# Two of every 32 tiles of gathered rows are replaced by column copies on VectorE and ScalarE

## The reference

```python
msg_in = concat([nodes[src], nodes[dst], edge_features])        # 64 + 64 + 32
messages = relu(msg_in @ mW1 + mb1) @ mW2 + mb2                 # 160 -> 128 -> 64
aggregated = segment_sum(messages, dst, num_segments=12500)
y = relu(concat([nodes, aggregated]) @ uW1 + ub1) @ uW2 + ub2   # 128 -> 128 -> 64
return layernorm(nodes + y)
```

## Time and profile before

| what | value |
|---|---|
| median of 3 runs | 2034.05 us |
| the profiled execution, its own time | 2035.36 us |
| its span | 2033.6 us |
| mean granted TensorE clock | 0.785 |
| busy: PE, DVE, ACT, POOL | 1408.9, 872.2, 557.6, 1488.3 us |
| DMA | 173.50 MB, 85 GB/s |

### The profile page before, as it was taken

The page is one execution under the profiler, slowest core; times in us unless marked ns, Lnnn a source line. Parts: engine busy times, 40 slices in busy tenths (PEclk is TensorE's granted clock), DMA queues, the critical chain, the costliest instruction groups (busy, mean ns, idle before and its releaser), DMA issues.

```text
span 2033.6 us, 34717 instructions
## 1 busy us (share of the span) xinstructions
PE 1408.9 (69%) x10080; PEld 1283.7 (63%) x10080; DVE 872.2 (43%) x2225; ACT 557.6 (27%) x928; POOL 1488.3 (73%) x1576
## 2 busy tenths in 40 slices
PE   6777767666667676666766676767676767767775
PEld 6766666566666666666665565656665656656664
DVE  3543333333333333333334444444444444544444
ACT  4322222222222222222222232333233333333332
POOL 1777777777777777777777777777777777777774
PEclk8876777777777877787777877887787788787877
DMA  9732223322322322232222322323232323322321
GB/s 233 226 87 78 78 77 81 80 77 78 81 77 78 82 79 77 78 81 80 77 77 72 80 79 76 80 77 81 77 80 78 80 75 81 79 78 75 82 80 43
DMA packets 167906, 173.50 MB, mean 85 GB/s; under 512 B 65718, under 2 KB 129497, under 8 KB 167785
## 3 DMA queue, kind: packets, MB, share of 16 engines
q0 software_dynamic: 50016, 102.53, 19.4%
q1 hardware_dynamic: 104168, 63.40, 11.2%
q10 hardware_dynamic: 13698, 7.28, 1.6%
HBM read 156.74 MB, written 16.31 MB: 85 GB/s over the span
## 4 chain that ended last, share of the span: by engine, by line
POOL 69%; issue 24%; DMA 3%; PE 2%; POOLq 1%; DVE 0%; ACT 0%; SPq 0%; DVEq 0%; ACTq 0%
POOL ag L227 69%; DMA src_table<-ag 1%; PE bank L375 1%; DMA dst_table<-picks 1%; POOLq L213 0%; POOLq L224 0%; POOLq L785 0%; DMA xc<-x_t 0%; DMA dst_table<-hid 0%; PE bank L264 0%; PE bank L642 0%; PE bank L648 0%; PE bank L274 0%; DMA ag<-src_table,slot_idx 0%; DMA picks<-edge_t 0%
## 5 line engine op out<-in xcount | busy, mean ns | idle before, releaser
L227 POOL DMA_INDIRECT ag<-src_table,slot_idx x1563 | 1481.7, 948 | 521.5 <-issue 475.7
L274 PE MATMUL bank<-oh,hid 128*128 128x96 f32 x3128 | 532.5, 325 | 421.9 <-DVE xc L333 378.1
L274 PEld LDWEIGHTS bank<-oh,hid 128*128 128x128 f32 x3128 | 478.2, 234 | 481.0 <-ACT hid L295 428.4
L316 DVE TENSOR_TENSOR hid<-bank,ag 128x512 f32<-128x512 f32 x391 | 270.4, 692 | 897.0 <-DMA ag<-src_table,slot_idx 769.8
L264 PE MATMUL bank<-picked,picks 128*128 128x128 f32 x3128 | 583.2, 346 | 5.9 <-DMA picks<-edge_t 5.4
L295 ACT ACTIVATE hid<-hid 128x512 f32<-128x512 f32 x391 | 245.8, 629 | 1175.0 <-DVE hid L316 1175.0
L264 PEld LDWEIGHTS bank<-picked,picks 128*128 128x128 f32 x3128 | 521.2, 252 | 9.5 <-issue 5.9
L289 ACT ACTIVATE picks<-bank 96x512 f32<-96x512 f32 x391 | 226.6, 580 | 173.6 <-PE bank L251 131.4
L303 DVE TENSOR_TENSOR oh<-iota,rel 128x384 f32<-128x384 f32 x391 | 217.8, 557 | 118.9 <-PE bank L278 64.2
L251 PE MATMUL bank<-ident_bf,oh 128*96 128x128 bf16 x1564 | 194.2, 261 | 53.3 <-DVE oh L303 52.7
L251 PEld LDWEIGHTS bank<-ident_bf,oh 128*96 128x96 bf16 x1564 | 147.8, 155 | 104.1 <-DVE oh L303 66.2
(11 more groups left out here) (57 smaller groups left out, 327.8 us busy)
## 6 DMA issues: line engine op xcount, KB each, us to landing
picks<-edge_t SPq DMA_DIRECT2D x391, 64.0 KB
ag<-src_table,slot_idx POOLq DMA_INDIRECT x1563
picked<-dst_table SPq DMA_DIRECT2D x391, 48.0 KB
src_table<-ag SPq DMA_DIRECT2D x25, 256.0 KB, 4.2
dst_table<-picks SPq DMA_DIRECT2D x17, 256.0 KB, 4.6
xc<-x_t ACTq DMA_DIRECT2D x8, 400.0 KB, 15.3
resid<-x_rows SPq DMA_DIRECT2D x24, 128.0 KB
out<-resid ACTq DMA_DIRECT2D x24, 128.0 KB
```

What stands on the lines that cost most here:

```text
L227: pool.indirect_dma_start(out=ag[:, k, j * DH:(j + 1) * DH], out_offset=None, in_=src_table, in_offset=bass.IndirectOffsetOnAxis(ap=slot_i ...
L274: nc.tensor.matmul(ps_a[q][:, 0:WIN], hid[:, q, j * DH:(j + 1) * DH], oh[:, r, j * WIN:(j + 1) * WIN], start=(j == 0), stop=(j == TPG - 1))
L316: dve.tensor_tensor(hid[:, q, :], ps_h[q][:, :], ag[:, k, :], ALU.add).then_inc(s_pre, 1)
```

## The change

In every lap after the first, the last 2 of the 4 tiles of group k = 5 are no longer gathered. Their 256 source nodes' columns of `xc` (64 floats each, a column on 64 partitions) are copied into a tile `own_x`, 32 columns in each of 8 steps: 12 by VectorE, 20 by ScalarE. A column is copied as 4 bytes a partition, at a byte offset from a register. TensorE multiplies `own_x` with the source part of `mW1`, two more products into the same PSUM bank, and VectorE's addition in that group covers only the two gathered tiles. The copies for a lap begin in step 5 of the lap before (3 steps, list `own_late`) and end in step 4 (5 steps, list `own_early`).

The lists come from the host's `src` as an additional input; VectorE multiplies them by 4 once, SyncE writes them to device memory at the start and fetches both lists each lap (640 and 384 bytes). VectorE's window positions are now read from a copy shifted by two elements, `base_lag2`, so that its load also begins at element 8·lap of an aligned row.

```diff
+OWN_K = 5
+OWN_TILES = 2
+OWN_AT = (TPG - OWN_TILES) * DH
+OWN = OWN_TILES * P
+OWN_N = OWN // UNROLL
+OWN_DVE = 12
+OWN_LATE = (UNROLL - OWN_K) * OWN_N
...
+        def load_own(sp, k, lap):
+            last = isinstance(lap, int) and lap == ITERS - 1
+            if k == 1 and not (isinstance(lap, int) and lap == 0):
+                sp.wait_ge(s_own_dve, (lap - 1) * UNROLL + 1)
+                sp.wait_ge(s_own_act, (lap - 1) * UNROLL + 1)
+                sp.dma_start(own_early[:, :], own_dram[ds(lap, 1), OWN_LATE:]).then_inc(s_own_early, 16)
+            if k == OWN_K - 1 and not last:
...
+                sp.dma_start(own_late[:, :], own_dram[ds(lap + 1, 1), 0:OWN_LATE]).then_inc(s_own_late, 16)
...
+        def own_columns(eng, et, k, lap, a, b, copy, s_done):
...
+            offsets = nc.values_load_multi_w_load_instructions(
+                row[0:1, at + a:at + b], engines=(et,), min_val=0, max_val=4 * (N_NODES - 1),
+                skip_runtime_bounds_check_because="four times the number of a node")[1]
+            for n, offset in enumerate(offsets):
+                c = step * OWN_N + a + n
+                done = copy(own_x[:, c:c + 1].bitcast(u8), xc[0:D, :].bitcast(u8)[:, ds(offset, 4)])
+            done.then_inc(s_done, 1)
+
+        def own_columns_dve(k, lap):
+            own_columns(nc.vector, ET.DVE, k, lap, 0, OWN_DVE, nc.vector.tensor_copy, s_own_dve)
+
+        def own_columns_act(k, lap):
+            def copy(to, of):
+                return nc.scalar.activation(to, of, ACT.Copy)
+            own_columns(nc.scalar, ET.Activation, k, lap, OWN_DVE, OWN_N, copy, s_own_act)
...
+            own = TPG - OWN_TILES if has_own(k, lap) else TPG
             for j in range(TPG):
                 last = nc.tensor.matmul(ps_h[q][:, j * DH:(j + 1) * DH], picks[:, r, j * P:(j + 1) * P],
-                                        picked[:, r, :], start=True, stop=True)
+                                        picked[:, r, :], start=True, stop=j < own)
+                if j >= own:
+                    if j == own:
+                        pe.wait_ge(s_own_dve, lap * UNROLL)
+                        pe.wait_ge(s_own_act, lap * UNROLL)
+                    last = nc.tensor.matmul(ps_h[q][:, j * DH:(j + 1) * DH],
+                                            own_x[:, (j - own) * P:(j - own + 1) * P],
+                                            w_src[0:D, :], start=False, stop=True)
             last.then_inc(s_h, 1)
...
+            if has_own(k, lap):
+                act.activation(hid[:, q, OWN_AT:], ps_h[q][:, OWN_AT:], ACT.Relu)
+                act.activation(hid[:, q, 0:OWN_AT], hid[:, q, 0:OWN_AT], ACT.Relu).then_inc(s_relu, 1)
+                return
...
-            dve.tensor_tensor(hid[:, q, :], ps_h[q][:, :], ag[:, k, :], ALU.add).then_inc(s_pre, 1)
+            w = OWN_AT if has_own(k, lap) else TPG * DH
+            dve.tensor_tensor(hid[:, q, 0:w], ps_h[q][:, 0:w], ag[:, k, 0:w], ALU.add).then_inc(s_pre, 1)
...
+            row, at = (base_lag2, start + 2) if eng is ET.DVE else (base_row, start)
...
             store_src_table(sp, range(4, 10))
-            sp.wait_ge(s_scratch, 64)
+            sp.wait_ge(s_own_4, 1)
+            sp.dma_start(own_dram, own_i).then_inc(s_scratch, 16)
+            sp.wait_ge(s_scratch, 80)
...
                         if exists(g):
-                            relu(g, k)
+                            relu(g, k, i)
+                        own_columns_act(k, i)
...
                             add_window(g - 2, (k - 2) % UNROLL, bases[k])
+                        own_columns_dve(k, i)
                         if c is not None:
                             if k == 1:
                                 dve_c2(c)
```

More of the change, by code:

```diff
@@ L53, in build @@
     bf16 = mybir.dt.bfloat16
+    u8 = mybir.dt.uint8
     ALU = mybir.AluOpType
@@ L125, in build @@
         oh = sb("oh", [P, RING, TPG * WIN])
+        own_late = sb("own_late", [1, OWN_LATE], i32)
+        own_early = sb("own_early", [1, OWN - OWN_LATE], i32)
+        own_x = sb("own_x", [D, OWN])
         hid = sb("hid", [P, 2, TPG * DH])
@@ L168, in build @@
         s_flag = sem("s_flag")
+        s_own = sem("s_own")
+        s_own_4 = sem("s_own_4")
+        s_own_late = sem("s_own_late")
+        s_own_early = sem("s_own_early")
+        s_own_dve = sem("s_own_dve")
+        s_own_act = sem("s_own_act")
         s_rel = sem("s_rel")
@@ L217, in upper_halves, with gathered_of, gathered_tiles, has_own @@
             return ap.bitcast(bf16).rearrange("p (n two) -> p n two", two=2)[:, :, 1]
+        def gathered_of(k, lap):
+            return 16 * TPG + lap * 16 * gathered_tiles(k)
+        def gathered_tiles(k):
+            return TPG - OWN_TILES * (k == OWN_K)
+        def has_own(k, lap):
+            return k == OWN_K and not (isinstance(lap, int) and lap == 0)
+        def load_own(sp, k, lap):
[5 more added lines that the diff above has]
+            if k == OWN_K - 1 and not last:
+                if not (isinstance(lap, int) and lap == 0):
+                    sp.wait_ge(s_own_dve, (lap - 1) * UNROLL + UNROLL - OWN_K)
+                    sp.wait_ge(s_own_act, (lap - 1) * UNROLL + UNROLL - OWN_K)
+                sp.dma_start(own_late[:, :], own_dram[ds(lap + 1, 1), 0:OWN_LATE]).then_inc(s_own_late, 16)
@@ new lines, in own_listed @@
+        def own_listed(eng, k, lap):
+            if k == OWN_K and not (isinstance(lap, int) and lap == ITERS - 1):
+                eng.wait_ge(s_own_late, (lap + 1) * 16)
+            elif k == 0 and not (isinstance(lap, int) and lap == 0):
+                eng.wait_ge(s_own_early, lap * 16)
+        def own_columns(eng, et, k, lap, a, b, copy, s_done):
+            step = (k - OWN_K) % UNROLL
+            last = isinstance(lap, int) and lap == ITERS - 1
+            if k >= OWN_K:
+                if last:
+                    return
+                row, at = own_late, step * OWN_N
+            else:
+                if isinstance(lap, int) and lap == 0:
+                    return
+                row, at = own_early, step * OWN_N - OWN_LATE
+            offsets = nc.values_load_multi_w_load_instructions(
[5 more added lines that the diff above has]
+            done.then_inc(s_done, 1)
@@ L289, in copy_oh, with relu @@
             act.activation(picks[0:WIN, r, :], ps_o[q][0:WIN, :], ACT.Copy).then_inc(s_oht, 1)
-        def relu(g, k):
+        def relu(g, k, lap):
             act = nc.scalar
@@ L312, in add_source @@
             missing = G_END * TPG - T_END if isinstance(g, int) and g == G_END - 1 else 0
-            wait(dve, s_gathered[k], (lap + 1) * 16 * TPG - 16 * missing)
+            wait(dve, s_gathered[k], gathered_of(k, lap) - 16 * missing)
             wait(dve, s_h, g + 1)
             wait(dve, s_agg, g - 1)
-            dve.tensor_tensor(hid[:, q, :], ps_h[q][:, :], ag[:, k, :], ALU.add).then_inc(s_pre, 1)
+            w = OWN_AT if has_own(k, lap) else TPG * DH
+            dve.tensor_tensor(hid[:, q, 0:w], ps_h[q][:, 0:w], ag[:, k, 0:w], ALU.add).then_inc(s_pre, 1)
         def next_indices(g, k):
@@ L335, in window_bases @@
         def window_bases(eng, start, n):
+            row, at = (base_lag2, start + 2) if eng is ET.DVE else (base_row, start)
             return nc.values_load_multi_w_load_instructions(
-                base_row[0:1, ds(start, n)], engines=(eng,), min_val=0, max_val=LAST_BASE,
+                row[0:1, ds(at, n)], engines=(eng,), min_val=0, max_val=LAST_BASE,
                 skip_runtime_bounds_check_because="the chip clamps them to this range")[1]
@@ L786, in windowed @@
                     for k in range(UNROLL):
-                        gather(pool, i * UNROLL + k, k)
+                        gather(pool, i * UNROLL + k, k, gathered_tiles(k))
                 for g in range((ITERS - 1) * UNROLL, G_END):
-                    gather(pool, g, g % UNROLL, min(TPG, T_END - g * TPG))
+                    gather(pool, g, g % UNROLL, min(gathered_tiles(g % UNROLL), T_END - g * TPG))
             windows_fit(pool, windowed, general_pool)
@@ L849, in lap @@
                             load_edges(sp, g, k)
+                        load_own(sp, k, i)
                 lap(0)
```

16 lines of the change are left out of this document (14 added, 2 removed).

## The result

| | before | changed kernel |
|---|---|---|
| median of 4 runs, us | 2034.39 | 2233.72 |
| lowest and highest, us | 2033.94 to 2036.25 | 2227.78 to 2236.15 |
| span of the profiled execution, us | 2033.6 | 2230.2 |
| mean granted TensorE clock | 0.785 | 0.741 |

The changed kernel takes 1.0974 times the time of before (95% interval 1.095 to 1.0997). Slower was forecast, and by the mechanism named VectorE does bound the laps with update. But 2109 us was forecast, with a range of 2000 to 2215; the loss is 199 us where 75 were said.

What follows compares the result with a forecast made beforehand. POOL's gathers bound the kernel; with the change VectorE would bound the laps with update. 2035.4 + 2 (start) - 62.5 (plain laps) + 131 (laps with update) + 4 (end) = 2109.9, so 2109 us; range 2000 to 2215.

Steps and rivals of the forecast that it cites:

- POOL's lap: Gathers on POOL: two of 32 go at 1.249 us each, so a lap falls from 39.97 to 37.47 us.
- the loads: Register loads at each step's start: 0.78 us for VectorE's 12 values, 1.19 for ScalarE's 20, aligned values four to a read.
- VectorE's step: One of 8 steps of a lap on VectorE: load and 12 copies add 2.04 us, 2.21 becomes 4.25.
- the lap with update: The 22 laps with update: VectorE bounds them at 45.93 us, over 39.97 by 5.96, +131 us in all.
- VectorE's branch back: End of VectorE's lap: the sum had no term of its own for the jump back to the loop's start.
- two waits for the update's products: VectorE idle for TensorE's two update products, 3.59 and 1.90 us before; no longer hidden, 5.4 us kept per lap with update.
- wait ahead of group 5: VectorE before L316 of group 5, after the last columns and three products: about 0.7 us a lap, an estimate.
- ScalarE's lag: Laps with update: ScalarE's square and root stand behind its own 20 columns, 0.6 us a lap.
- 8 steps: VectorE's steps of a lap at 4.25 us each: 34.0 us.
- the update's own parts: VectorE's update work in a lap with update: 0.42, 0.75, 1.57 and 1.34 us, in sum 4.08.
- lap's end without the branch: VectorE from L333 to L303, with window positions loaded from an aligned row: 1.14 us, added as 1.15.
- The fetch: Rival: longer loops fetch instructions each lap; VectorE pays 3 us a lap, 2209 us in all; chance 0.12.

Runs made afterwards that it cites:

- e_keep: Changed kernel, but all 32 tiles are gathered again while the columns are still copied and multiplied; 2300.29 us.
- f2_fill: Changed kernel plus 60 small memsets on VectorE, run once ahead of its loop with update, which moves that loop; 2165.26 us, 1.0645 of before.
- e_act1: Changed kernel, but ScalarE copies only the first of its 20 columns of a step and loads one offset; 2228.93 us, 1.0953 of before.
- f2_order: Changed kernel with VectorE's columns behind the update's part of each step, and ScalarE's columns and relu reordered too; 2095.53 us, 1.029 of before.
- e_plain: Changed kernel with the change in laps 1 to 25 only; laps with update gather all 32 tiles and copy no columns; 1989.30 us, 0.9777 of before.
- f2_best: Changed kernel with one tile as columns instead of two in laps with update, columns behind the update's parts; 1980.27 us, 0.9730 of before.
- g_best: As f2_best, plus unused TensorE products ahead of its waits for the update's two products; 1988.63 us, 0.9762 of before.

## Why the prediction was wrong

The steps that held: POOL's lap, 37.47 forecast and 37.91 measured, where the term that was off is the gather's duration, taken as the 0.944 us of before and now 0.966; the loads, 0.78 forecast and 0.85 measured for 12 values, 1.19 and 1.26 for 20, so aligned values come four to a read and not one; VectorE's step, 4.25 and 4.11; ScalarE, which the forecast kept below VectorE and which costs nothing; VectorE as the bound of the laps with update, where `e_keep` shows the gathers to be worth nothing. Of the four loads in the earlier trace rows the one of 6 aligned values, 0.843, would by that reading be two reads, 0.54. It fits if the last two values take a read each, three reads like the 12 values' 0.848.

The step that failed is the lap with update, 45.93 us forecast and 51.01 measured. The sum put VectorE's branch back at nothing and the waits for TensorE's products at their size of before:

| term | forecast | measured |
|---|---|---|
| VectorE's branch back | 0 | 3.38 (`f2_fill`) |
| two waits for the update's products | 5.4 | 4.10 + 3.45 = 7.55 |
| wait ahead of group 5 | 0.7 | 2.00 |
| ScalarE's lag | 0.6 | 0 (`e_act1`) |
| 8 steps | 34.0 | 8 x 4.11 = 32.9 |
| the update's own parts | 4.08 | 0.34 + 0.78 + 1.57 + 1.32 = 4.0 |
| lap's end without the branch | 1.15 | 1.35 (`f2_fill`: 1205.05 - 1199.59 - 4.11) |

The differences are +3.38, +2.15, +1.3, -0.6, -1.1, -0.1 and +0.2: 5.2 us, where the laps lost 5.1. The fetch was written down as a rival with a chance of 0.12 and 3 us a lap. Its price was right and its place too broad: it came in one of VectorE's loops, the one on the bound. It was weighed against the 12 packets of today's loops, which say nothing on loops three to thirteen times as long. And it was added to the forecast's lap as it stood (2209 us), though it adds to whatever the waits come to. With it the sum is 2109 + 22 x 3.38 = 2183 us; the other 50 are the waits (some 37) and the plain laps (11).

The waits for the products were taken from the earlier trace rows as they stood. But the first product was slow there since TensorE had been idle for 4.01 us, and the second fast behind 1.44. The change puts about 2 us of columns in front of the instruction that releases each (from the last L428 to L759 2.16 us instead of 0.29, to L767 2.26 instead of 0.18). TensorE is then idle for 3.03 us before the second product too, and that product nearly doubles. A row's duration at the higher clock was carried over to a place where TensorE is idle for longer and the clock is the lower one. That the columns stand ahead of the releasing instruction was seen in the order, and no price was put on it. `f2_order` shows 5.69 us for the other order, more than the 2.15 by which the waits were mis-sized, since it takes back part of the forecast's 5.4 as well.

## What to carry to other kernels

Read a price together with the state it was taken in: here a TensorE product behind 3 to 4 us of idle time mostly took 2.05 to 2.07 us instead of 1.10, so whatever delayed its releaser cost once for the delay and once for the clock. Put new work behind the instruction that another engine waits for, not ahead of it. When a loop grows by hundreds of instructions, count the branch back as a term of its own (3.4 us here), beside and not instead of the others, and look in the profile after for instruction packets and for a wait whose named releaser had already ended. And where two phases of a loop have different slack, spend it only where it is: `e_plain` is 0.978 of before, the full change 1.097.

## What the runs showed of the hardware that I had not expected

- A loop of 295 rows on VectorE pays about 3.3 us at its branch back at one place in the instruction list and 0.23 at another, 60 instructions on. ScalarE's loop of 370 rows went the other way when moved by 78, from 0.2 to 2.5 us.
- ScalarE and VectorE issue copies of one column with an address from a register at 0.096 (20 in 2.01 us) and 0.106 us each, the register instruction included; each lasts 0.19 and 0.165 us, so they overlap.
- A load of registers took 0.60 (8 values), 0.85 (12) and 1.26 us (20) from aligned addresses, and 1.84 (8) two elements off. 6 aligned values took 0.84, as much as 12.
- The mean duration of a gather differs from kernel to kernel: 0.944 us before, 0.966 in the plain laps of the changed kernel, 0.977 and 0.990 in `f2_best` and `g_best`, with the median at 0.944. At 31 gathers a lap that is 1.0 and 1.4 us.
